# A four-layer decoder on one core: head sums of the narrow attentions sent through DRAM batch by batch, and the last stage's weights built earlier

## The chip, the core and the metric

The kernel runs on one core of a Trainium2 chip. Its engines are TensorE (PE, with its weight load PEld), VectorE (DVE), ScalarE (ACT), GpSimd (POOL) and SyncE (SP), which here issues the transfers. Each engine works through its own instructions in order and waits on semaphores. The metric is the device time of one execution, in microseconds.

## The reference, cut to what matters

Four layers of three sublayers each update `x` (8 batches, 256 tokens, 128 features); every sublayer gets a layer norm of `x` and adds to it. Four of the twelve are attentions with 16 heads of 8 features: two over a context of 512 keys and two causal ones over 256 keys, the last of them gated. All four end like this one, and the last sublayer is a chain of three low-rank-adapted, quantised blocks:

```python
def _L3_xattn_ref(query, key, value, mask, Wq, Wk, Wv, Wo, Wg, bg):
    ...
    scores = jnp.einsum('bhqd,bhkd->bhqk', q, k) / jnp.sqrt(jnp.float32(dk))
    ...
    attn = jax.nn.softmax(scores, axis=-1)
    context = jnp.einsum('bhqk,bhkd->bhqd', attn, v)
    context = context.transpose(0, 2, 1, 3).reshape(B, Sq, D)
    gate = jax.nn.sigmoid(query @ Wg.T + bg)
    return gate * context @ Wo.T

def _L3_ffn_ref(x, qweights, scales, biases, lora_a, lora_b, ln_gamma, ln_beta):
    ...
    h = x
    for blk in range(3):
        i0, i1 = (2 * blk, 2 * blk + 1)
        y = _qlora_linear(h, qweights[i0], scales[i0], biases[i0], lora_a[i0], lora_b[i0])
        y = _layernorm(y, ln_gamma[blk], ln_beta[blk])
        y = jax.nn.gelu(y, approximate=False)
        y = _qlora_linear(y, qweights[i1], scales[i1], biases[i1], lora_a[i1], lora_b[i1])
        h = y + h
    return h
```

## The kernel before, in words

`x` stays in on-chip memory with the features on the partitions and 2048 tokens in columns, worked on as four tiles of 512 columns or eight batches of 256. Each sublayer is one or more blocks of instructions; no engine starts the next block before all have ended the one before.

A narrow attention (`narrow_attention`, L3043) is three stages. `project` (L730) norms `x`, projects queries, keys and values (`unit`), splits them into bf16 parts and stores the first ones in DRAM; at its end SyncE loads the first batch's stacks, while TensorE runs 24 filler matmuls (`keep_clock`). Then `attend_wide` (512 keys, L1151) or `attend_short` (256 keys, L1327) runs nine steps: step s scores batch s ("front") and turns batch s - 1 into logits, exponentials and head sums ("back"). A step goes over the 16 heads, i = 0 to 15. VectorE reduces each score matrix to row maxima. Half a batch's maxima are turned by TensorE, copied by ScalarE and written as further rows of the query stack by two transfers (`place`, L1012 and following); TensorE waits for them at i = 0 and i = 8 (`attend_halves`). SyncE's order in a step is written out in `attend_transfers` (L998): second half of this batch's loads, row maxima, first half of the next batch's loads, row maxima. The sums of four heads make one group; a column group of 32 rows holds a head's eight weighted values and, in the ninth row, the sum of its exponentials. They are copied into `summed`.

After all nine steps `combine` (L1797) handles all eight batches at once: it gathers the denominators by matmuls with constant matrices, inverts them (`reciprocal` of 256 columns, after a guard against zero in the gated stage), gathers the numerators, spreads the inverses, multiplies, and in the gated stage makes the gates (a matmul, a sigmoid and a product on GpSimd), and last it projects and adds to `x`, tile by tile.

The last stage, `lora_ffn` (L2848), loads its weights, dequantises them on GpSimd, builds six 128 x 128 matrices on TensorE (`centre_lora`, `weights`) between and after its norm's steps, and then runs three blocks. In a block each phase goes over all four tiles: `up` into y, ScalarE's squares of all tiles, one square root, one reciprocal, the products z, then per tile a transpose, the Gelu and `down`, and the residual add; the next block's `up` start when all `down` have been issued.

## Time and the profile before

| quantity | value |
|---|---|
| median of 3 runs | 1738.42 us (1737.92 to 1742.84) |
| the profiled execution's own time | 1742.06 us |
| its span | 1740.3 us |
| granted TensorE clock, mean | 0.916 of 2.4 GHz |
| busy | PE 84%, DVE 58%, ACT 46%, POOL 26% |

The span runs from the first to the last instruction of one profiled execution; all times in rows are microseconds from its start unless they say ns. A timeline row has start, length, engine, source line, operation, output and input, count, and in brackets the idle time before it and what ended it. Rows of matmuls count fp32 ones twice. A row of a stretch has its bounds and length, then the busy time and count of PE, PEld, DVE, ACT and POOL, TensorE's granted clock as a share of 2.4 GHz, the share of time that the DMA engines were busy, and the data rate in GB/s.

### The profile page before, as it was taken

To read this page: it belongs to the slowest core of one execution; us is meant where nothing else is said; L and a number is where in the kernel's file an instruction comes from. 1 tells how busy PE (TensorE), PEld (TensorE's weight loads), DVE (VectorE), ACT (ScalarE), POOL (GpSimd) and SP (SyncE) were. 2 spreads that over 40 slices of the span, in tenths; PEclk is the share of its full clock that TensorE was granted. 3 is DMA by queue.
4 is the path that set the end of the run, shared out by engine and by line. 5 is a ranking of instruction groups with operands and counts; after the bars stand their busy time and mean duration, and the time that the engine had idled before them with its cause. 6 is when DMAs were issued, how large, how long until landed. Compare 5 with 4: busy or idle time off the path is not lost. (4 is left out here: it accounts for less than half of the span.)

```text
span 1740.3 us, 30717 instructions
## 1 busy us (share of the span) xinstructions
PE 1470.2 (84%) x10727; PEld 738.2 (42%) x10747; DVE 1009.0 (58%) x1970; ACT 797.1 (46%) x1479; POOL 455.9 (26%) x658
## 2 busy tenths in 40 slices
PE   7998999999749999679876898889836888888887
PEld 5777634444424445246533442222404333433354
DVE  5665598884352222465547578997274574567335
ACT  3554537677213333215330136777434365346535
POOL 6121300000144443320126230000003354245311
PEclk9999999999969999699887898999957899989878
DMA  2000443110200000001000163121001520342000
GB/s 95 1 0 0 146 161 93 42 49 8 117 0 0 1 0 0 0 7 49 5 6 0 57 198 110 50 54 29 15 0 44 169 70 21 98 157 66 11 16 24
DMA packets 82246, 85.67 MB, mean 49 GB/s; under 512 B 7228, under 2 KB 67900, under 8 KB 81756
## 3 DMA queue, kind: packets, MB, share of 16 engines
q1 hardware_dynamic: 82152, 84.45, 15.2%
q8 instruction: 55, 0.90, 0.2%
q14 instruction: 39, 0.32, 0.1%
HBM read 51.33 MB, written 32.51 MB: 48 GB/s over the span
## 5 line engine op out<-in xcount | busy, mean ns | idle before, releaser
L1282 ACT ACTIVATE arena<-ps 128x1024 f32<-128x1024 f32 x256 | 261.9, 1023 | 112.1 <-PE ps L1191 111.2
L1176 PE MATMUL ps<-k_stack,q_stack 49*128 49x512 bf16 x512 | 192.3, 387 | 15.3 <-DVE small L1306 13.2
L1191 PE MATMUL ps<-q_stack,k_stack 51*128 51x256 bf16 x1024 | 191.3, 275 | 0.5 <-ACT arena L1282 0.4
L1303 DVE CUSTOM_DVE_ANT_0 small<-ps,mask_b 128x512 bf16<-128x512 f32 x256 | 168.0, 689 | 33.7 <-PE ps L1176 32.3
L1306 DVE TENSOR_REDUCE small<-ps 128x1 f32<-128x512 f32 x256 | 162.1, 685 | 22.6 <-PE ps L1176 21.6
L1492 DVE TENSOR_REDUCE small<-ps 128x6 f32<-128x768 f32 x128 | 122.6, 958 | 77.8 <-PE ps L1374 75.7
L1203 PE MATMUL ps<-arena,v_pad 128*32 128x256 f32 x2048 | 163.7, 394 | 1.1 <-ACT arena L1282 1.1
L1468 ACT ACTIVATE arena<-ps 128x384 f32<-128x384 f32 x256 | 117.8, 488 | 76.5 <-PE ps L1393 75.8
L1076 POOL TENSOR_SCALAR_AFFINE_SELECT arena<-arena 128x256 f32<-128x256 f32 x256 | 101.9, 406 | 84.2 <-ACT arena L1468 84.0
L2543 DVE TENSOR_TENSOR arena<-ps,arena 128x512 f32<-128x512 f32 x64 | 44.3, 692 | 120.8 <-PE ps L2509 120.8
L2558 POOL TENSOR_TENSOR arena<-arena 128x512 f32<-128x512 f32 x64 | 80.9, 1264 | 108.9 <-DVE arena L2543 107.1
L1183 PE MATMUL ps<-mask_b,ident_b 64*128 64x512 bf16 x512 | 99.8, 382 | 0.5
L1176 PEld LDWEIGHTS ps<-k_stack,q_stack 49*128 49x128 bf16 x512 | 47.7, 94 | 113.2 <-DVE small L1306 82.2
L1049 POOL TENSOR_TENSOR small<-small 128x16 bf16<-128x16 f32 x64 | 13.8, 216 | 312.6 <-DVE small L1309 286.7
L1191 PEld LDWEIGHTS ps<-q_stack,k_stack 51*128 51x128 bf16 x1024 | 75.4, 95 | 29.2 <-issue 6.8
L223 PE MATMUL ps<-xT,mean_w 128*128 128x512 f32 x96 | 56.0, 737 | 24.2 <-DMA xT<-in_xT 4.5
L945 POOL TENSOR_TENSOR arena<-arena 128x512 bf16<-128x512 f32 x40 | 45.5, 1157 | 113.9 <-ACT arena L852 113.9
L238 ACT ACT_TABLE_LOAD x14 | 18.0, 1283 | 113.8 <-PEq L1569 26.2
L2531 ACT ACTIVATE arena<-ps 128x512 f32<-128x512 f32 x64 | 38.2, 597 | 68.9 <-PE ps L2505 65.8
L2505 PE MATMUL ps<-xn,arena 128*128 (+1 forms) x128 | 66.9, 605 | 2.4 <-PEq L2407 2.0
L2490 PE MATMUL ps<-arena 128*128 128x512 f32 x128 | 65.1, 595 | 1.9 <-POOL arena L2558 1.9
L2509 PE MATMUL ps<-xn,arena 128*128 (+1 forms) x128 | 66.3, 599 | 0.0
(353 smaller groups left out, 3036.2 us busy)
## 6 DMA issues: line engine op xcount, KB each, us to landing
q_stack<-q_scratch SPq DMA_DIRECT2D x128, 96.0 KB
k_stack<-k_scratch SPq DMA_DIRECT2D x64, 192.0 KB
k_scratch<-arena SPq DMA_DIRECT2D x8, 768.0 KB, 3.6
k_stack<-k_scratch SPq DMA_DIRECT2D x64, 96.0 KB
q_scratch<-arena SPq DMA_DIRECT2D x4, 1152.0 KB, 5.4
arena<-in_ctxT SPq DMA_DIRECT2D x8, 512.0 KB, 6.6
k_scratch<-arena SPq DMA_DIRECT2D x8, 512.0 KB, 4.7
k_scratch<-arena SPq DMA_DIRECT2D x16, 256.0 KB, 4.5
```

Source lines behind the costliest of these rows:

```text
L1076: pool.affine_select(diag, diag, [[0, 2], [1, P]], ALU.is_ge, 0.0, 0, -1).then_inc(g["masked"].sem, 1)
L1176: pe.matmul(ps[:, t, :], c.q_stack[par][64 * e:64 * e + ROW_MAX, pr, t * P:(t + 1) * P], c.k_stack[par][64 * e:64 * e + ROW_MAX, pr, :], s ...
L1183: return pe.matmul(ps[:, 2 + 2 * (i % 2) + half, :], c.ident_b[r, :], c.mask_b[r, m:m + 2 * S], start=first, stop=False, skip_group_check= ...
L1191: mm = pe.matmul(ps[:, bank, (ch % 2) * S:(ch % 2 + 1) * S], c.k_stack[prv][64 * e:64 * e + ROWS, pr, ch * P:(ch + 1) * P], c.q_stack[prv] ...
L1203: mm = pe.matmul(ps[32 * j:32 * j + 32, 6 + grp % 2, 0:S], c.v_pad[par][:, piece, head_of(i), :], buf.probs[i % 8][:, piece * S:(piece + 1 ...
L1282: act.activation(buf.probs[i % 8], ps[:, bank:bank + 2, :].rearrange("p a n -> p (a n)"), ACT.Exp, scale=scale).then_inc(g["probs"].sem, 1)
L1303: dve.tensor_tensor_reduce(buf.junk[t], ps[:, t, :], c.mask_b[:, M_X + t * SC:M_X + (t + 1) * SC], 1.0, FLOOR, op0=ALU.add, op1=ALU.max, a ...
L1306: dve.tensor_reduce(out, ps[:, t, :], X, ALU.max).then_inc(g["maxed"].sem, 1)
L1468: act.activation(buf.probs[i % 8][:, 0:3 * P], ps[:, 4 + i % 2, 0:3 * P], ACT.Exp, scale=scale)\
L1492: dve.tensor_reduce(buf.m3[par][:, hf, :, pr % HALF, :], ps[:, bank:bank + 2, 0:3 * P].rearrange("p e (a n) -> p e a n", a=3), X, ALU.max)\
L2505: pe.matmul(ps[:, 2 + n % 2, :], w13[:, (ex * 4 + j) * P:(ex * 4 + j + 1) * P], x, start=True, stop=True)\
L2558: pool.tensor_tensor(acts[n % 4][:, :], gated[n % 2][:, :], share_e[n // 2 % 2][:, :], ALU.mult)\
```

## The change

`combine` goes. The head sums of a batch are stored in DRAM as soon as they are complete, with all 32 rows of a head, and come back in another layout: numerators as 128 rows of 256, denominators as 128 rows of 32 columns. VectorE inverts the latter, they are stored again and spread to all rows of a head. These five transfers a batch are issued by SyncE within the attention's steps. From step 4 on ("late") the quotient, the gate, the projection and the add of batch s - 4 lie within step s; in the wide stages the product is on GpSimd and the add goes by way of ScalarE and GpSimd. The last three batches are handled after the steps (`finish_pe`, `finish_act`, `finish_dve`), batch 7 by matmuls instead of transfers. The gate's matmuls and sigmoids move to the end of the projecting stage. The last stage's weights are loaded and built there too (`LoraWeights`), and its three blocks are interleaved tile by tile, with the square root and the reciprocal in two halves. The head order of the output weights and the layout of the constants follow; constants that are needed late are loaded apart. The diff, cut to its core (`LoraWeights.weights` and `dequantise` are as in `lora_ffn` before):

```diff
+            if gated:
+                for t in TS:
+                    if t < 2:
+                        pe.wait_ge(g["ln_scaled"].sem, g["ln_scaled"].at(4))
+                    else:
+                        pe.wait_ge(g["gate_out"].sem, g["gate_out"].at(t - 1))
+                    pe.matmul(ps[:, 2 + t % 2, :], w[:, W_G:W_G + P], norm.tile(c.xn, t), start=True, stop=True)\
+                      .then_inc(g["gate_in"].sem, 1)
+            if ahead:
+                ahead.turn(pe)
...
+            if gated:
+                for t in TS:
+                    act.wait_ge(g["gate_in"].sem, g["gate_in"].at(t + 1))
+                    act.activation(norm.tile(c.xn, t), ps[:, 2 + t % 2, :], ACT.Sigmoid, bias=w[:, W_BG:W_BG + 1])\
+                       .then_inc(g["gate_out"].sem, 1)
+            if ahead:
+                ahead.keep(act)
...
+        with nc.Fori(2, B // 2, 1, engines=[engine]) as it:
+            body(it, 0, True, True, True, True)
+            body(it, 1, True, True, True, True)
+    body(B // 2, 0, False, True, True, True)
...
+    def store_sums(self, buf, sp, b):
+        c, g = self.c, self.c.sig
+        for i in range(2):
+            sp.wait_ge(g[f"summed_out{i}"].sem, g[f"summed_out{i}"].at(2 * b + 2))
+        sp.dma_start(c.sum_scratch[b, :, :, :].rearrange("r j m -> j r m"), buf.summed[:, b, :, :].rearrange("p k n -> p (k n)")).then_inc(g["sums_stored"].sem, 16)
...
+    def spread(self, sp, out, src, sem):
+        sp.dma_start(out, src.unsqueeze(0).to_broadcast([DH, H, S])).then_inc(sem, 16)
...
+    def load_sums(self, sp, b, last=False):
+        c, g = self.c, self.c.sig
+        sem = g[f"sums_back{b % 2}"].sem
+        sp.wait_ge(g["sums_stored"].sem, g["sums_stored"].at(16 * (b + 1)))
+        if b > 1:
+            done, n = self.quotient(b - 2)
+            sp.wait_ge(done.sem, done.at(n + 1))
+        sp.dma_start(self.num[b % 2], c.sum_scratch[b, 0:DH, :, :].rearrange("d j (k n) -> (d j k) n", n=S)).then_inc(sem, 16)
+        if last:
+            self.spread(sp, self.rec[b % 2], c.sum_scratch[b, DH, :, :].rearrange("j (k n) -> (j k) n", n=S), sem)
+        else:
+            sp.dma_start(self.den[b % 2], c.sum_scratch[b, DH, :, :].rearrange("j (a n) -> (j a) n", a=P // 4)).then_inc(sem, 16)
+    def store_inverse(self, sp, b):
+        c, g = self.c, self.c.sig
+        sp.wait_ge(g["inverted"].sem, g["inverted"].at(b + 1))
+        sp.dma_start(c.inv_scratch[b, :, :].rearrange("q (a n) -> (q a) n", a=P // H), self.den[b % 2]).then_inc(g["inv_stored"].sem, 16)
+    def spread_inverse(self, sp, b):
+        c, g = self.c, self.c.sig
+        sp.wait_ge(g["inv_stored"].sem, g["inv_stored"].at(16 * (b + 1)))
+        self.spread(sp, self.rec[b % 2], c.inv_scratch[b, :, :], g[f"inv_spread{b % 2}"].sem)
+    def invert(self, dve, par, half, b):
+        g = self.c.sig
+        dve.wait_ge(g[f"sums_back{par}"].sem, g[f"sums_back{par}"].at(32 * half + 32))
+        if self.guard:
+            dve.tensor_scalar(self.den[par], self.den[par], 1e-30, None, ALU.max).then_inc(g["den_fixed"].sem, 1)
+            dve.wait_ge(g["den_fixed"].sem, g["den_fixed"].at(b + 1))
+        dve.reciprocal(self.den[par], self.den[par]).then_inc(g["inverted"].sem, 1)
+    def divide(self, eng, par, half, done="quotient"):
+        g = self.c.sig
+        eng.wait_ge(g[f"inv_spread{par}"].sem, g[f"inv_spread{par}"].at(16 * half + 16))
+        eng.tensor_tensor(self.quot[par], self.num[par], self.rec[par], ALU.mult).then_inc(g[done].sem, 1)
+    def gate(self, pool, par, b):
+        c, g = self.c, self.c.sig
+        done, n = self.quotient(b)
+        pool.wait_ge(done.sem, done.at(n + 1))
+        pool.tensor_tensor(self.quot[par], self.quot[par], c.xn[:, bass.ds(b * S, S)], ALU.mult).then_inc(g["gated"].sem, 1)
+    def project(self, pe, par, b, bank):
+        c, g = self.c, self.c.sig
+        done, n = (g["gated"], b) if self.gated else self.quotient(b)
+        pe.wait_ge(done.sem, done.at(n + 1))
+        pe.matmul(c.ps[:, bank, 0:S], self.w[:, W_O:W_O + P], self.quot[par], start=True, stop=True, skip_group_check=True)\
+          .then_inc(g["out_proj"].sem, 1)
...
+    def finish_pe(self, buf, pe, scored):
+        c, g = self.c, self.c.sig
+        pe.wait_ge(g["maxed"].sem, g["maxed"].at(scored))
+        pe.wait_ge(g["probs"].sem, g["probs"].at(H * B))
+        self.project(pe, 1, B - 3, 0)
+        self.project(pe, 0, B - 2, 1)
+        for k in range(GROUPS):
+            out = g[f"summed_out{k % 2}"]
+            pe.wait_ge(out.sem, out.at(2 * B - 1 + k // 2))
+            den = pe.matmul(c.ps[0:H, 3, 0:S], c.consts[:, C_DEN + 12 - 4 * k:C_DEN + 12 - 4 * k + H], buf.summed[:, B - 1, k, :],
+                            start=(k == 0), stop=(k == GROUPS - 1), skip_group_check=True)
+            if k == GROUPS - 1:
+                den.then_inc(g["den"].sem, 1)
+            num = pe.matmul(c.ps[:, 4, 0:S], c.consts[:, C_NUM + 3 - k:C_NUM + 3 - k + P], buf.summed[:, B - 1, k, :],
+                            start=(k == 0), stop=(k == GROUPS - 1), skip_group_check=True)
+        num.then_inc(g["num"].sem, 1)
+        keep_clock(c, pe, 6, bank=2)
+        pe.wait_ge(g["inverted"].sem, g["inverted"].at(B))
+        pe.matmul(c.ps[:, 5, 0:S], c.consts[0:H, C_ROWS:C_ROWS + P], self.rec[1][0:H, :], start=True, stop=True, skip_group_check=True)          .then_inc(g["den_spread"].sem, 1)
+        self.project(pe, 1, B - 1, 2)
...
+        def inverse(par, b, rows, den):
+            rec = self.rec[par][0:rows, :]
+            if self.guard:
+                dve.tensor_scalar(rec, den, 1e-30, None, ALU.max).then_inc(g["den_fixed"].sem, 1)
+                dve.wait_ge(g["den_fixed"].sem, g["den_fixed"].at(b + 1))
+                den = rec
+            dve.reciprocal(rec, den).then_inc(g["inverted"].sem, 1)
+        self.divide(dve, 1, B // 2 - 2, "last_quotient")
+        self.add(dve, B - 3, 0)
+        dve.wait_ge(g["sums_back0"].sem, g["sums_back0"].at(16 * B))
+        inverse(0, B - 2, P, self.rec[0])
+        dve.wait_ge(g["inverted"].sem, g["inverted"].at(B - 1))
+        dve.tensor_tensor(self.quot[0], self.num[0], self.rec[0], ALU.mult).then_inc(g["last_quotient"].sem, 1)
+        self.add(dve, B - 2, 1)
+        dve.wait_ge(g["den"].sem, g["den"].at(1))
+        inverse(1, B - 1, H, c.ps[0:H, 3, 0:S])
+        dve.wait_ge(g["num_kept"].sem, g["num_kept"].at(1))
+        dve.wait_ge(g["den_spread"].sem, g["den_spread"].at(1))
+        dve.tensor_tensor(self.quot[1], c.ps[:, 5, 0:S], self.num[1], ALU.mult).then_inc(g["last_quotient"].sem, 1)
+        self.add(dve, B - 1, 2)
...
+        if s > 2:
+            outs.store_inverse(sp, s - 3)
+        if s > 1:
+            outs.store_sums(buf, sp, s - 2)
...
+        if s > 1:
+            outs.load_sums(sp, s - 2, s == B)
+        if s > 2:
+            outs.spread_inverse(sp, s - 3)
...
+        if late and not causal:
+            outs.divide(pool, par, it - 2)
...
+            if late and outs.gated and i == 4:
+                outs.gate(pool, par, s - 4)
...
+        if late and not causal:
+            pool.wait_ge(g["out_kept"].sem, g["out_kept"].at(s - 3))
+            xb = c.xT[:, bass.ds((s - 4) * S, S)]
+            pool.tensor_tensor(xb, xb, outs.kept[par], ALU.add).then_inc(g["residual"].sem, 1)
...
+                    if late and i == 7:
+                        project_late(c, outs, pe, s, par)
...
+                    if late and i == 7:
+                        act.wait_ge(g["out_proj"].sem, g["out_proj"].at(s - 3))
+                        act.activation(outs.kept[par], ps[:, 7, 0:S], ACT.Identity, bias=outs.w[:, W_BO:W_BO + 1])\
+                           .then_inc(g["out_kept"].sem, 1)
...
+                    if n == 2 and s > 2:
+                        outs.invert(dve, 1 - par, (s - 3) // 2, s - 3)
...
+                    if late and pr == 1:
+                        outs.divide(dve, par, it - 2)
+                    if (late or par) and before and pr == 2:
+                        outs.invert(dve, 1 - par, it - 2 + par, s - 3)
+                    if late and pr == 3:
+                        outs.add(dve, s - 4, 7)
...
+class LoraWeights:
...
+    def turn(self, pe):
+        c, g = self.c, self.c.sig
+        pe.wait_ge(g["centring"].sem, g["centring"].at(1))
+        pe.wait_ge(g["lora_in"].sem, g["lora_in"].at(48))
+        pe.wait_ge(g["gate_out"].sem, g["gate_out"].at(T // NT))
+        for i in range(NB):
+            c_matmul(pe, c.ps[:, 2, i * P:(i + 1) * P], self.cols[:, 2 * i:2 * i + 1].to_broadcast([P, P]), self.centring)
+            mm = c_matmul(pe, c.ps[0:LR, 3, i * P:(i + 1) * P], self.turned_up[:, i, :], self.centring)
+        mm.then_inc(g["lora_centred"].sem, 1)
+        pe.wait_ge(g["dequant"].sem, g["dequant"].at(2))
+        pe.wait_ge(g["lora_kept"].sem, g["lora_kept"].at(2))
+        pe.wait_ge(g["ln_std"].sem, g["ln_std"].at(4))
+        self.weights(pe, 0, 4, 4)
+        self.weights(pe, 4, NL, 2)
+    def keep(self, act):
+        c, g = self.c, self.c.sig
+        act.wait_ge(g["lora_centred"].sem, g["lora_centred"].at(1))
+        act.activation(self.up_shift.rearrange("p a n -> p (a n)"), c.ps[:, 2, 0:NB * P], ACT.Identity).then_inc(g["lora_kept"].sem, 1)
+        act.activation(self.up_b[0:LR, :, :].rearrange("p a n -> p (a n)"), c.ps[0:LR, 3, 0:NB * P], ACT.Identity)\
+           .then_inc(g["lora_kept"].sem, 1)
+        for n, i0, i1, bank in ((1, 0, 4, 4), (2, 4, NL, 2)):
+            act.wait_ge(g["turned"].sem, g["turned"].at(n))
+            act.activation(self.wT[:, i0:i1, :].rearrange("p a n -> p (a n)"), c.ps[:, bank, 0:(i1 - i0) * P], ACT.Identity)
...
+            def turn(n, t):
...
+            norm_pe(norm, pe, follow=lambda t: up(0, t))
...
+                for t in range(3):
+                    turn(NTI * blk, t)
+                down(blk, 0)
+                turn(NTI * blk, 3)
+                for t in range(1, 4):
+                    down(blk, t)
+                    if blk < NB - 1:
+                        up(blk + 1, t - 1)
+                if blk < NB - 1:
+                    up(blk + 1, 3)
...
+                    if t % 2:
+                        act.wait_ge(g["ln_square"].sem, g["ln_square"].at(NTI + n + t + 1))
+                        act.activation(half(dev, t // 2), half(ssq, t // 2), ACT.Sqrt, bias=c.consts[:, C_EPS:C_EPS + 1],
+                                       scale=1.0 / D).then_inc(g["ln_std"].sem, 1)
...
+                    residual(blk, t)
+                    if blk < NB - 1 and t:
+                        shift(blk + 1, t - 1)
+                if blk < NB - 1:
+                    shift(blk + 1, 3)
```

## Rows read from the trace of the kernel before

**Rows 1.** Busy time by stretch: third attention's `combine`, and the last stage.

```profile
1470.80:1487.50 16.70, 14.12 (x120) 6.20 (x120) 7.12 (x9) 2.39 (x4) 0.00 (x0) 0.90 0.00 0
1664.70:1740.30 75.60, 60.84 (x283) 42.59 (x284) 33.91 (x88) 38.57 (x135) 7.36 (x6) 0.81 0.07 23
```

**Rows 2.** Busy time by stretch: half steps, masked and unmasked wide; a whole short step.

```profile
312.00:324.90 12.90, 12.85 (x148) 5.38 (x148) 10.73 (x33) 8.99 (x11) 1.05 (x3) 1.00 0.17 46
...
1118.70:1130.00 11.30, 10.24 (x117) 3.29 (x117) 10.22 (x18) 8.78 (x11) 1.05 (x3) 1.00 0.19 53
...
1592.70:1605.60 12.90, 10.94 (x156) 4.41 (x148) 9.16 (x17) 8.25 (x21) 7.51 (x21) 1.00 0.22 64
```

**Rows 3.** Timeline around the first attention's `combine`.

```profile
439.20 1.93 PE L1203 MATMUL ps<-arena,v_pad 128*32 128x256 f32 x32 [0.55 <-ACT arena L1282]
...
445.61 1.76 DVE L1882 RECIPROCAL arena<-ps 128x256 f32<-128x256 f32 x1 [29.85 <-PE ps L1820]
...
455.95 0.75 DVE L1873 SCALAR_TENSOR_TENSOR xT<-ps,att_w,xT 128x512 f32<-128x512 f32 x1 [0.51 <-PE ps L1854]
```

**Rows 4.** Timeline around the gated attention's `combine`.

```profile
1637.56 0.65 PE L1408 MATMUL ps<-arena,v_pad 128*32 128x128 f32 x8
...
1648.21 1.28 ACT L1865 ACT_TABLE_LOAD   x1
...
1652.27 0.69 ACT L1865 ACTIVATE arena<-ps,att_w 128x512 f32<-128x512 f32 x1 [0.17 <-PE ps L1838]
...
1659.03 1.27 POOL L1897 TENSOR_TENSOR arena<-arena 128x512 f32<-128x512 f32 x1 [2.38 <-DVE arena L1886]
...
1663.71 0.75 DVE L1873 SCALAR_TENSOR_TENSOR xT<-ps,att_w,xT 128x512 f32<-128x512 f32 x1 [1.44 <-PE ps L1854]
```

**Rows 5.** Timeline of the gated attention's projecting stage, its end.

```profile
1509.68 5.13 PE L184 MATMUL ps<-mask_b,ident_b 128*128 128x512 bf16 x23
...
1511.29 0.63 ACT L852 ACTIVATE arena<-arena 128x512 bf16<-128x512 f32 x1 [0.37 <-DVE arena L898]
...
1518.49 0.59 PE L184 MATMUL ps<-mask_b,ident_b 128*128 128x512 bf16 x2 [3.69 <-PEq L770]
```

**Rows 6.** Timeline of two norms: a bare one, and the start of another.

```profile
460.33 5.37 PE L223 MATMUL ps<-xT,mean_w 128*128 128x512 f32 x8 [4.42 <-PEq L2398]
...
472.88 0.69 DVE L269 TENSOR_TENSOR xn<-arena,ps 128x512 f32<-128x512 f32 x1 [0.20 <-PE ps L205]
...
1487.59 3.67 PE L223 MATMUL ps<-xT,mean_w 128*128 128x512 f32 x8 [1.11 <-PEq L1811]
```

**Rows 7.** Timeline of the last stage: the building of its weights.

```profile
1674.93 2.23 PE L205 MATMUL ps<-arena 128*128 128x128 f32 x12
...
1677.59 0.46 ACT L2957 ACTIVATE arena<-ps 32x384 f32<-32x384 f32 x1
...
1691.37 0.39 PE L2907 MATMUL ps<-arena 128*128 128x128 f32 x2
...
1694.70 0.60 ACT L2962 ACTIVATE arena<-ps 128x512 f32<-128x512 f32 x1 [0.26 <-PE ps L2908]
```

**Rows 8.** Timeline of the last stage: its three blocks.

```profile
1688.05 0.69 DVE L3003 TENSOR_TENSOR arena<-ps,arena 128x512 f32<-128x512 f32 x1 [1.02 <-PE ps L205]
...
1694.76 3.23 DVE L3010 TENSOR_SCALAR arena<-arena,small 128x128 f32<-128x128 f32 x16
...
1709.46 0.25 DVE L3006 RECIPROCAL small<-small 128x16 f32<-128x16 f32 x1 [2.51 <-ACT small L2982]
...
1726.43 0.25 DVE L3006 RECIPROCAL small<-small 128x16 f32<-128x16 f32 x1 [2.50 <-ACT small L2982]
...
1736.69 0.75 DVE L3017 SCALAR_TENSOR_TENSOR xT<-ps,arena,xT 128x512 f32<-128x512 f32 x1 [0.39 <-PE ps L2950]
```

**Rows 9.** The page's DMA issues, and SyncE's own in the gated steps.

```profile
k_scratch<-arena SPq DMA_DIRECT2D x16, 256.0 KB, 4.5
...
L960 SPq DMA_DIRECT2D k_stack<-k_scratch x24: 443/446/1080, 1541.3 to 1613.8; - x24
```

More of the change, by code:

```diff
@@ L951, in project @@
         g.advance(**{f"ctx_in{t}": 16 for t in TS})
+    if gated:
+        g.advance(gate_in=T // NT, gate_out=T // NT)
+    if ahead:
+        ahead.advance()
 def load_stacks(c, sp, par, hf, q_at, k_at, nk, key_mask_at=None):
@@ L1058, in attend_pool, with step @@
     pool.wait_ge(g["cleared"].sem, g["cleared"].at(1))
-    def step(it, par, front, back, before):
+    def step(it, par, front, back, before, late):
         s = it * 2 + par
@@ L1207, in sum_piece, with step @@
                     mm.then_inc(g["summed"].sem, 1)
-            def step(it, par, front, back, before):
+            def step(it, par, front, back, before, late):
                 first = isinstance(it, int) and it == 0
@@ L1313, in _ @@
                 step(s)
+            outs.invert(dve, 1, B // 2 - 2, B - 3)
+            outs.finish_dve(dve)
+    outs.advance()
+    g["out_kept"].advance(B - LAST)
     if masked:
@@ L1394, in logits, with sum_piece @@
                       .then_inc(g["logits"].sem, 1)
-            def sum_piece(grp, piece, b, par, first, front=True):
+            def sum_piece(grp, piece, b, par, first, front=True, late=False):
                 if piece == 0:
-                    sum_waits(c, pe, grp, b, first, front, "masked")
+                    sum_waits(c, pe, grp, b, first, front, late, "masked", "residual")
                 for j in range(4):
@@ L1410, in sum_piece, with step @@
                     mm.then_inc(g["summed"].sem, 1)
-            def step(it, par, front, back, before):
+            def step(it, par, front, back, before, late):
                 first = isinstance(it, int) and it == 0
@@ L2852, in lora_ffn @@
+def lora_ffn(c, weights):
     nc, g, ps = c.nc, c.sig, c.ps
@@ L2994, in _, with shift, residual @@
         def _(dve):
-            dve.tensor_tensor(centring, c.ident[:, :], c.mean_w[:, :], ALU.subtract).then_inc(g["centring"].sem, 1)
+            def shift(blk, t):
+                dve.wait_ge(g["up"].sem, g["up"].at(NTI * blk + t + 1))
+                dve.tensor_tensor(fold(y[:, t, :], (4, P)), fold(ps[:, t, :], (4, P)),
+                                  up_shift[:, blk, :].unsqueeze(1).to_broadcast([P, 4, P]), ALU.add).then_inc(g["y_kept"].sem, 1)
+            def residual(blk, t):
+                dve.wait_ge(g["down"].sem, g["down"].at(NTI * blk + t + 1))
+                if blk == NB - 1:
+                    dve.wait_ge(g["summed"].sem, g["summed"].at(t + 1))
+                h = norm.tile(c.xT if blk == NB - 1 else c.xn, t)
+                dve.scalar_tensor_tensor(h, ps[:, t, :], cols[:, 2 * blk + 1:2 * blk + 2], h, ALU.add, ALU.add)\
+                   .then_inc(g["residual"].sem, 1)
```

429 lines of the change are left out of this document (173 added, 256 removed).

## The prediction

> **What bounds the kernel now.** The profiled execution took 1742.06 us (span 1740.30); the median of the runs is 1738.42. The sum below is made in the frame of the profile and its difference is carried over to the median. The page's chain of waits reaches back only through the last stage, so I read stages instead: the boundaries from the timeline, then busy time by stretch, then single rows. The reader should see four attention stages with a serial tail (`combine`) and a last stage that nothing overlaps. Within the attention loops TensorE is the bound: in half a step of the masked wide loop it is busy 12.85 of 12.90 us, in half a step of the unmasked one 10.24 of 11.30 with VectorE at 10.22, in a whole step of the short one 10.94 of 12.90 [rows 2]. In the tails the bound is a chain that hops between engines: the `combine` of the third attention holds 16.7 us in which TensorE's records cover 14.1 but VectorE 7.1 and ScalarE 2.4 [rows 1]; the last stage, 75.6 us, has no engine over 61 us, at a granted clock of 0.81 [rows 1].
>
> **The change, part by part.**
>
> *1. The tails.* Now: from the end of the last head-sum matmuls (439.20 + 1.93 = 441.1) to the last residual add (455.95 + 0.75 = 456.7), 15.6 us in a wide stage [rows 3]; about 17.3 in the third attention (the window of 16.7 and a good half us of copy ahead of it) [rows 1]; 1638.2 to 1664.5, 26.3 us, in the gated one [rows 4]. After: batches 0 to 4 leave within the loop, and `finish_pe` and `finish_dve` handle three. Its order matters. TensorE projects batch 5, VectorE adds it, and only then does VectorE invert batch 6's 256 columns; a reciprocal of 256 columns costs 1.76 us whatever the rows [rows 3]. `finish_pe` issues the projection of batch 6 ahead of batch 7's eight sum matmuls, so those wait for it although their data is there. One full-width fp32 matmul of 512 columns takes 3.67 / 4 = 0.92 us at full clock, close to 0.86 start to start, so one of 256 takes 0.43 [rows 6]. Chain: projection 0.65 with its latency, add 0.4 (half of 0.75), reciprocal 1.76, product 0.45: 3.3 us. Nine matmuls: 3.9. Then reciprocal 1.76, spread 0.65, product 0.45, projection 0.65, add 0.4: 3.9. Sum 11.1 us at full clock.
> But TensorE is idle for nearly 3 us in the first piece. After 4.42 us idle the norm's eight matmul records took 5.37 us, after 1.11 us idle 3.67 [rows 6]: the stretch began at 1.2 GHz. I add the same 1.7 us to the nine matmuls and 0.3 for the second gap, under the last reciprocal: 13.1 us per tail. (The Trainium skill, TensorE: Matmul & The Clock Gate, What's actually happening, says that the throttled state is the default and activity releases it; by it the six filler matmuls, which come only after the sums, can't help those sums. By that rule the tail is 13.1, without it 11.1.) Saved: 2.5 in each wide stage, 5 in all, between 4 and 9. Third attention: 17.3 - 13.7 (batch 5's spread reciprocals may land half a microsecond late) = 3.5, between 1 and 5.5. Gated: 13.7, two guards at about 0.45 and two Pool gates of 256 columns at half of 1.27 plus a handover [rows 4], 16.1; saved 10, between 8 and 13. Gate matmuls and sigmoids are gone from it. Sum of part 1: 18.5.
> The norm after the third attention now starts 1.11 us after dense matmuls and runs at full clock. After the change it follows a sparse tail: +1.7 (5.37 - 3.67) [rows 6]. The other norms start at half clock already.
>
> *2. In the loops.* In four steps per stage that also score, TensorE gets a projection of 256 columns: 0.43, where it is the bound. ScalarE's extra 256-column copy and Pool's product and add in the wide loops hide in their slack (ScalarE 8.8 of 11.3, Pool 1.1 [rows 2]). VectorE gets one reciprocal of 32 columns per step: between 0.25 (16 columns) [rows 8] and 1.76 (256), by the slope 0.35; in the short loops a product and an add of 0.4 each too, under a busy time of 9.1 of 12.9 [rows 2]. In the unmasked loop both engines stand near 10.2 of 11.3, and part of it shows. In the short loops Pool also gates (0.65) ahead of the masking that the sums wait for. I take 0.5 us a step: 2 us a stage, 8 us in all; from 4 (half of TensorE's share hides) to 14 (every addition of TensorE and VectorE shows).
> The five transfers a batch cost SyncE five issues of about 0.45 us [rows 9]. In the gated short loop it has twelve loads and four row-maximum transfers a step, 9.1 us by the same row and its waits, so 11.4 with the new ones, of a step of at most 12.9 [rows 2]: just under. The data (512 KB out, some 290 KB back, twice as much as half a step's loads) meets DMA engines busy 0.22 of the time [rows 2]; a landing is 4.5 us [rows 9], and each has a third of a step or more. I cost them at nothing; the cover is the order of SyncE's queue. Without it, batch sums come late to VectorE's in-order reciprocal, and what is late next is the reduce behind it and so the scores.
>
> *3. The gated projecting stage.* It now ends when SyncE has issued its loads: TensorE ends its filler at 1514.8 and waits 3.69 us for the block's end, until 1518.5 [rows 5]. That slack is all the cover. The new work stands in TensorE's queue ahead of the 24 filler matmuls, and they stay. ScalarE is done at 1511.9 [rows 5]. Table load and four sigmoids with their matmuls: 1648.21 to 1652.96, 4.75 us [rows 4], to 1516.7. Twelve small matmul records 2.2 and two copies, 3.1 us (1674.9 to 1678.05) [rows 7], to 1519.8. Weights: four of them 3.4 us at full clock (1691.3 to 1694.7), 0.85 each [rows 7]; I take six at 1.07, partly at half clock, 6.4, to 1526.2. Filler 5.3 (5.13 for 23) [rows 5], to 1531.5. Block end and next start, 0.4: 1531.9 against 1518.5. Cost +13.4; all at full clock 12, with half clock throughout the weights and gates 17. The five weight transfers are issued in SyncE's idle time after the context's, and Pool's dequantising ends before its first part is due: nothing. All of the next stage shifts, since its own transfers are issued from its start.
>
> *4. The last stage.* Norm: centring and weights are gone from it. A bare norm runs from 460.33 to 473.6, 13.2 us [rows 6]; with the four `up` (0.93 each) woven in between its products, VectorE's first shift ends at +16.5 after the stage's start. Now it ends at 1688.74 - 1664.74 = +24.0 [rows 8]. Saved 7.5. Blocks: now 17.0 from reciprocal to reciprocal (1709.46 to 1726.43) and 15.0 for the first pair; the last add ends at 1737.44 [rows 8]. After: from a block's first shifted tile, two tiles of squares 2.6, square root 0.3, reciprocal 0.25; the other two squares go on, so the second root ends at +5.5 to 6.0 instead of all before the one root; table load and first Gelu input 1.5, at +7.5; Gelu 0.78; `down` 0.93 and residual 0.75, then `up` 0.93 and shift 0.7 for tile 0: the next block's first shifted tile at +12.7. The z products (3.23 for 16 [rows 8]) of the first half are now under the squares. Three blocks: 12.7 + 12.7 + 12.8 = 38.2; after 16.5, the end at +54.7 against +72.7: 18 saved if TensorE has its full clock. It idles some 4 us in every block, and its turns can go at half clock; I take off 2: 16 saved, between 12 and 18.
>
> *5. The rest.* Later constants, split loads and one more unrolled pair of steps: nothing, the load is not waited for where it stands.
>
> **Sum.** 18.5 + 16 - 8 - 1.7 - 13.4 = 11.4 us less: 1742.06 - 11.4 = 1730.7 in the profile's frame, 1727 against the median of 1738.42. 0.3% (5.2 us) is about what a measurement of this kernel can tell from no change.
>
> **Rivals.**
> A (slower): *the transfers share one in-order queue with the row maxima.* TensorE waits for each batch's maxima at every half step. If the stores or SyncE's waits push those back, every step from the third on pays. From 0.6 us a step in all 28 steps, or 1.2 in the 14 short ones, the 11.4 are gone and the time is over 1743.6. At 1 us each: 1727 + 28 = 1755. For it: short steps leave SyncE only about 1.5 us. Against: no DMA wait in a steady step of the masked loop (12.85 busy of 12.90) and a DMA share near 0.2 [rows 2]. (The Trainium skill, DMA: Bandwidth & Descriptors, on the fixed part of a transfer, gives about 2.0 us; four dependent ones would be an estimated 8 us and more, which two steps hold.) Chance 0.13.
> B: *the projecting stage costs what the last stage gives.* Weights and gates at half clock (17), blocks at 14.5 us each (12 saved): 7.6 less gained, 1734.5, no measurable change. Chance 0.18.
> C: *cheap everywhere.* Loops 4, tails at full clock, projecting 12: 1714. For it: the short loops' slack. Chance 0.14.
> D: *the tails don't shrink*, because the first three-batch chain waits on transfers of the last step (each some 4 us): 3 us more in each, 1739. Chance 0.05.
> Forecast as summed, 1720 to 1733: 0.50.
> Range: from near C to between D and A, 1714 to 1741. Faster 0.68 (forecast, C, part of B), same 0.18, slower 0.14.
>
> **What the profile after would show.** The l3x attention begins 12 to 17 us later after its projecting stage starts, with matmuls of the last stage's weights and then the filler ahead of it. Tails of about 13 us in wide stages, 16 in the gated one, with a TensorE gap of some 3 us under a 1.76 us reciprocal. Late steps 0.3 to 0.8 us longer. The last stage 57 to 60 us to its end. I am wrong if row-maximum transfers appear as releasers in steady steps, if VectorE's 32-column reciprocal waits on a DMA, or if the projecting stage ends with SyncE as before.

## Result: 7.1% slower, and the profile after

The changed kernel takes 1861.63 us (median of 4 runs, 1859.1 to 1866.2), the kernel before 1738.17 us beside it (4 runs). The ratio is 1.071, with a 95% interval of 1.0678 to 1.0743. Forecast were 1727 us, within 1714 to 1741.

Where the 124.2 us between the two profiled spans (1864.5 and 1740.3) arise, by the first transfer or matmul of each stage in the timelines; two later kernels stand beside them:

| stage | before | after | difference | after, store in four (e1) | before with the last stage's part, no filler (e6) |
|---|---|---|---|---|---|
| start to the first wide attention | 180.1 | 182.2 | +2.1 | 182.1 | 182.1 |
| first wide attention, masked | 276.9 | 283.2 | +6.3 | 280.3 | 279.4 |
| stages up to the second | 532.8 | 535.7 | +2.8 | 535.0 | 529.5 |
| second wide attention | 257.7 | 269.5 | +11.8 | 256.8 | 255.9 |
| quantised block | 76.3 | 77.3 | +1.0 | 74.5 | 74.6 |
| third attention (short steps) | 163.7 | 216.7 | +52.9 | 172.9 | 166.5 |
| gated attention (short steps) | 177.2 | 239.1 | +61.9 | 196.2 | 176.8 |
| last stage | 75.6 | 60.9 | -14.6 | 60.4 | 59.9 |

The last stage did what was forecast. 115 us are lost in the two stages with short steps. By stretches, columns as in [rows 1] (four short steps of the third attention; the gated projecting stage; the last stage to its last add):

```profile
1433.20:1514.50 81.30, 60.15 (x602) 21.82 (x605) 39.96 (x75) 33.55 (x80) 31.00 (x85) 0.75 0.32 81
1564.40:1613.00 48.60, 43.93 (x188) 26.32 (x188) 14.87 (x29) 20.25 (x35) 11.41 (x10) 0.86 0.31 93
1803.50:1861.97 58.47, 48.11 (x240) 33.47 (x240) 33.62 (x90) 37.26 (x134) 5.09 (x4) 0.86 0.03 12
```

A short step holds 20.3 us where [rows 2] had 12.90 at most, and no engine is busy for more than 15.04 (60.15 / 4) of them, at a granted clock of 0.75. The work has not grown by 7 us; something is waited for. In these four steps TensorE waits 16.8 us in all for row maxima, four waits of at most 5.2; and behind them it runs for a while at the lower of its two clock levels, so that a wait costs more than it lasts: with the same work its busy time is 11.64 us a step in e1 below, at a granted clock of 1.00, against 15.04 here. TensorE's largest entry in the list of waits of the whole span (total, times, longest), and SyncE's largest from 1455 to 1580, the end of the third attention:

```profile
PE ps L1594 <- DMA q_stack<-max_rows: 50.0, 10, 7.4
```

```profile
SPq L1072 <- DMA sum_scratch<-arena: 21.3, 5, 9.4
SPq L1578 <- PEq L1578: 17.9, 1, 17.9
SPq L1212 <- ACT max_rows L1326: 16.0, 5, 6.2
SPq L1082 <- DVE small L1097: 7.1, 4, 1.8
```

TensorE's entry is the row maxima, which the prediction named as a sign that it was wrong, and which rival A was about. SyncE's timeline of one short step:

```profile
1474.13 1.29 SPq L1212 DMA_DIRECT2D q_stack<-max_rows  x2
1477.23 0.34 SPq L1082 DMA_DIRECT2D inv_scratch<-small  x1
1477.68 0.57 SPq L1058 DMA_DIRECT2D sum_scratch<-arena  x1
1479.42 0.31 SPq L992 DMA_DIRECT2D q_stack<-q_scratch  x1
1479.78 2.07 SPq L992 DMA_DIRECT2D k_stack<-k_scratch  x1
1481.90 1.10 SPq L992 DMA_DIRECT2D q_stack<-q_scratch  x1
1483.04 0.73 SPq L992 DMA_DIRECT2D k_stack<-k_scratch  x1
1483.82 1.29 SPq L1212 DMA_DIRECT2D q_stack<-max_rows  x2
1488.40 0.34 SPq L1072 DMA_DIRECT2D arena<-sum_scratch  x1
1488.79 0.43 SPq L1076 DMA_DIRECT2D small<-sum_scratch  x1
1489.26 0.67 SPq L1062 DMA_DIRECT2D arena<-inv_scratch  x1
...
1494.32 1.29 SPq L1212 DMA_DIRECT2D q_stack<-max_rows  x2
```

The reader is to see three things. The store of the sums (L1058) is issued at 1477.68, and SyncE, which waits for its landing at L1072, gets on at 1488.40, 10.7 us later. The load issues right behind the store take up to 2.07 us instead of 0.45: something holds up the queue. And the row-maximum pairs are 9.7 and 10.5 us apart instead of some 6.3. So there were two candidates: the store itself, and SyncE's dependent waits.

### The profile page after: what moved, and what is told of

The parts are those of the page before. It is cut to its first block and busy times, and to the rows that moved or that the text cites. A ratio compares the mean times of both kernels' runs of the same rounds, so it can differ in the third digit from the quotient of the medians.

```text
span 1864.5 us, 29754 instructions
## 1 busy us (share of the span) xinstructions
PE 1534.1 (82%) x10419; PEld 752.1 (40%) x10419; DVE 1024.5 (55%) x2020; ACT 795.4 (43%) x1480; POOL 473.5 (25%) x682
## 5 line engine op out<-in xcount | busy, mean ns | idle before, releaser
L1509 ACT ACTIVATE arena<-ps 128x1024 f32<-128x1024 f32 x256 | 262.2, 1024 | 126.4 <-PE ps L1415 126.1
L1400 PE MATMUL ps<-k_stack,q_stack 49*128 49x512 bf16 x512 | 193.9, 389 | 21.2 <-DVE small L1538 11.9
L1415 PE MATMUL ps<-q_stack,k_stack 51*128 51x256 bf16 x1024 | 193.0, 276 | 0.5 <-ACT arena L1509 0.4
L1538 DVE TENSOR_REDUCE small<-ps 128x1 f32<-128x512 f32 x256 | 163.7, 686 | 31.1 <-PE ps L1400 29.6
L1594 PE MATMUL ps<-mask_b,ident_b 128*128 128x256 bf16 x256 | 62.5, 336 | 66.7 <-DMA q_stack<-max_rows 50.0
L1250 POOL TENSOR_TENSOR small<-small 128x16 bf16<-128x16 f32 x64 | 13.8, 216 | 310.9 <-DVE small L1543 286.3
L1630 PE MATMUL ps<-q_stack,k_stack 51*128 51x256 bf16 x256 | 77.6, 346 | 0.0
L1613 PE MATMUL ps<-k_stack,q_stack 49*128 49x256 bf16 x256 | 75.0, 333 | 0.0
```

The source lines that it names most:

```text
L1400: pe.matmul(ps[:, t, :], c.q_stack[par][64 * e:64 * e + ROW_MAX, pr, t * P:(t + 1) * P], c.k_stack[par][64 * e:64 * e + ROW_MAX, pr, :], s ...
L1415: mm = pe.matmul(ps[:, bank, (ch % 2) * S:(ch % 2 + 1) * S], c.k_stack[prv][64 * e:64 * e + ROWS, pr, ch * P:(ch + 1) * P], c.q_stack[prv] ...
L1509: act.activation(buf.probs[i % 8], ps[:, bank:bank + 2, :].rearrange("p a n -> p (a n)"), ACT.Exp, scale=scale).then_inc(g["probs"].sem, 1)
L1538: dve.tensor_reduce(out, ps[:, t, :], X, ALU.max).then_inc(g["maxed"].sem, 1)
L1630: pe.matmul(ps[:, bank, 0:S], k[:, 0:P], q, start=True, stop=True, skip_group_check=True)
```

## The experiments

Ratios are to the kernel before on the same chip, with their 95% intervals in brackets.

**e1 and e2: the same data in four stores.** The single store has a destination pattern of 4 x 32 x 1024, with the 4 slowest.

```diff
-        sp.dma_start(c.sum_scratch[b, :, :, :].rearrange("r j m -> j r m"), buf.summed[:, b, :, :]...)
+        for j in range(4):
+            sp.dma_start(c.sum_scratch[b, 0:32, j, :], buf.summed[32 * j:32 * j + 32, b, :, :]...)
```

(e2 has 16 in place of 32 rows: half the bytes, all that is read back.)

> The changed kernel, with the 512 KB store of a batch's head sums issued as four transfers of 32 rows of 4 KB instead of one whose slowest dimension is 4; same bytes, same place in SyncE's order, same waits. Theory 1 (the single store is worked on by few DMA engines, so it lands only some 10.7 us after its issue, and SyncE, which waits for that landing ahead of the next loads and row maxima, passes the delay on): the store lands in about 4 us, the steps of the two short loops fall from 20.6 us to 14 to 15, the whole to 1765 to 1790. Theory 2 (the length of the dependent chain of waits in SyncE's queue, whatever the store): steps stay at 19 to 21, the whole above 1840. Theory 3 (the number of bytes): no change but three more issues of 0.45 us, about 1865.

> As the run with four stores of 32 rows, but only the first 16 rows of each head's 32 are stored (nine are read back): half the bytes. Theory 1: within 10 us of the run with 32 rows, 1755 to 1785. Theory 2: above 1840 like that one. Theory 3 (bytes): half of the loss of the two short loops comes back against the run with 32 rows, about 1810.

Measured: e1 1764.35 us, 1.0142 [1.0027, 1.0257]; e2 1764.98 us, 1.0145 [1.0043, 1.0248]. By the medians some 97 of the 124 us are gone (e1's interval alone leaves 20 us either way; e8 and e14, built on it, come out at 1.0161 and 1.0137) with the same bytes, the same place in the queue and the same waits, and half the bytes change nothing more. Theories 2 and 3 fall. SyncE's timeline of a short step in e1, and four of its steps by stretch:

```profile
1441.01 1.28 SPq L1213 DMA_DIRECT2D q_stack<-max_rows  x2
1442.39 0.34 SPq L1073 DMA_DIRECT2D arena<-sum_scratch  x1
...
1447.47 1.29 SPq L1213 DMA_DIRECT2D q_stack<-max_rows  x2
1449.72 0.34 SPq L1083 DMA_DIRECT2D inv_scratch<-small  x1
1450.17 1.77 SPq L1059 DMA_DIRECT2D sum_scratch<-arena  x4
1452.05 0.37 SPq L992 DMA_DIRECT2D q_stack<-q_scratch  x1
1452.46 0.46 SPq L992 DMA_DIRECT2D k_stack<-k_scratch  x1
...
1454.98 1.28 SPq L1213 DMA_DIRECT2D q_stack<-max_rows  x2
```

```profile
1413.50:1468.60 55.10, 46.55 (x608) 18.75 (x600) 40.31 (x77) 33.69 (x81) 30.88 (x84) 1.00 0.48 113
```

SyncE no longer waits for the landing (L1073 follows the row maxima at once, and a store's landing is 2.2 us by the page), load issues are back at 0.45, the clock is 1.00 and the step 13.8 us.

**e3, e4, e9, e10: the store alone, in the kernel before.** Each adds one transfer of 512 KB a step behind `place(s - 1, 1)`, of columns of x that don't change; nothing waits for it before the stage's end. Only the shape of the destination differs.

```diff
             place(s - 1, 1)
+        if s > 1:
+            sp.dma_start(c.sum_scratch[s - 2, :, :, :].rearrange("r j m -> j r m"), c.xT[:, 0:GROUPS * S])...
```

> The kernel before, with one more transfer a step from step 2 on: 512 KB to DRAM, with the changed kernel's access pattern (slowest dimension 4), right behind the row maxima of the second half; it stores columns of x that nothing changes here, and nothing waits for it. Theory 1 in its narrow form (only SyncE's wait for the landing counts): no more than 2 us a short step for a fuller queue, 1742 to 1760. Theory 1 in its wide form (row maxima and loads use the same few DMA engines and queue up behind the store even without a wait): 5 us or more in each of 14 short steps, above 1800. Theory 2: 1740 to 1745.

> The same added transfer to the kernel before, but with 128 rows as its slowest dimension. By either form of theory 1: 1738 to 1750, well under the run whose slowest dimension is 4 if the wide form holds. If bytes count (theory 3): as long as that run.

> The kernel before with the same added 512 KB transfer a step that nothing waits for, its destination pattern now of 8 x 16 x 1024 with the 8 slowest. If the slowest dimension sets how many DMA engines work on a transfer, it lands in about half the time of the one with 4, some 5 us, and costs the short steps little: 1738 to 1760, against 1806 with 4. If it is the permuted order of the rows in DRAM that makes it slow, as much as with 4: about 1806.

> As that run, with 16 x 8 x 1024 and the 16 slowest: permuted like the pattern with 4, but divisible by 16. If the slowest dimension decides: the landing is near the 2.7 us of the unpermuted store and the time that of the kernel before, 1733 to 1745. If the permuted order decides: about 1806.

| slowest dimension of the destination | time, us | ratio | landing by the page |
|---|---|---|---|
| 4 (e3) | 1806.11 | 1.0382 [1.0277, 1.0487] | none given |
| 8 (e9) | 1757.03 | 1.0094 [1.0064, 1.0124] | none given |
| 16, rows permuted (e10) | 1746.03 | 1.0028 [1.0007, 1.0048] | 3.7 us |
| 128, rows in order (e4) | 1736.70 | 0.9986 [0.9946, 1.0026] | 2.7 us |

The same 512 KB cost 66 us, 16, 5 or nothing (the ratio less one, times 1739), by the pattern alone. The interval of the 66 reaches from 48 to 85 us, and those of the last two rows overlap, so that a price of the permuted order by itself is not shown. (e10 missed its range of 1733 to 1745 by 1 us and its landing of 2.7 by 1.) The rest goes with the slowest dimension. How the DMA engines work on it, in 30 us of short steps (the row DMA is their mean busy share in 40 slices, in tenths), e3 first, then e4:

```profile
DMA  2555324268000000001226135562245811000000
...
sum_scratch<-xT SPq DMA_DIRECT2D x1, 512.0 KB
```

```profile
DMA  4957800000076200029506730000007630007900
...
sum_scratch<-xT SPq DMA_DIRECT2D x2, 512.0 KB, 2.7
```

With 4 slowest the engines are about a quarter to a half busy on average over 7 to 11 us at a time; with 128, in bursts of two to five slices that reach 0.9, with idle time between. TensorE in e3 waits for the same transfers as in the changed kernel (list of waits, four and a half short steps):

```profile
PE ps L1360 <- DMA q_stack<-max_rows: 9.7, 3, 4.0
...
PE ps L1360 <- DMA k_stack<-k_scratch: 7.4, 1, 7.4
```

Read together: a few engines carry the whole store, and the row maxima, 4 KB a transfer, and the loads come to lie behind it. The delay without any wait is measured; that it comes from shared engines is the reading that fits the table and the DMA rows. (The Trainium skill, DMA: Bandwidth & Descriptors, Why a DMA increments its semaphore by 16 and not by 1, says that a transfer issued by SyncE runs on the largest number of engines up to 16 that divides the slowest dimension of both its patterns, and on the lowest-numbered ones. By it the store has four engines, and the row maxima, whose destination has two rows slowest, two of the same four. The order 4, 8, 16 of the table agrees; which engine carried what no run here shows.) It would have been the rule to weigh in the prediction.

**e12: the wait for the landing, by itself.** e3, and SyncE waits for the store's landing behind `place(s, 0)`, where the changed kernel does.

```diff
+        if s > 1:
+            sp.wait_ge(g["sums_stored"].sem, g["sums_stored"].at(16 * (s - 1)))
```

> The kernel before with the added 512 KB store whose slowest dimension is 4 (1806 without a wait), and SyncE waits for its landing behind the row maxima of the first half, where the changed kernel does. If the wait is the other part of the loss of the short loops (their steps: 20.6 us in the changed kernel, 17.0 with the store alone), steps near 20 and 1830 to 1850. If the wait is nearly free because the queue is held up anyway: 1806 to 1815, and the rest of the changed kernel's loss is its own work and its other transfers.

Measured: 1804.17 us, 1.0359 [1.0307, 1.0411], like e3. So the wait is nearly free here, and by the reading above it should be: the row maxima placed just before it lie behind the same store, so TensorE would wait in any case. With e3's 66 us without any wait, the narrow form of my theory is refuted. But the wait is shorter here than in the changed kernel: 6.7 us in four and a half short steps (1400 to 1480) against 13.5 in four (1433.2 to 1514.5), where the store is issued later. That the longer one is free too is not shown.

**e13, e14, e15: the rest of the short loops.** By the medians e3 explains 66 us and e1 leaves 25; 33 of 124 are still open. e13 (the changed kernel) and e14 (e1) move the store of the reciprocals behind the row maxima; e15 adds to e3 two reads a step that nothing waits for, shaped like those of the numerators and of the spread reciprocals.

```diff
-        if s > 2:
-            outs.store_inverse(sp, s - 3)
         if s > 1:
             outs.store_sums(buf, sp, s - 2)
 ...
             place(s, 0)
+        if s > 2:
+            outs.store_inverse(sp, s - 3)
```

> The changed kernel with its single store, but the store of the reciprocals (for which SyncE waits on VectorE) stands behind the row maxima of the first half instead of ahead of the store of the sums. If that wait (the store of the sums is issued 3.5 us after the row maxima in the changed kernel, 1.3 us in the kernel before with the store added) holds up the whole queue: 1 to 2 us less in each of 14 short steps, 1835 to 1850. If the reads and the broadcast behind the store are the rest: within 5 us of 1862.

> The same move in the version with four stores of 32 rows (1764). There no engine waited for a transfer in steady short steps, so the order in the queue shouldn't count: 1760 to 1768. If SyncE's wait still held up row maxima: 1745 to 1755.

> The kernel before with the added store whose slowest dimension is 4 (1806), and behind the first half's row maxima two reads that nothing waits for: 128 KB with 128 rows slowest, and a broadcast of 16 KB to 128 rows, whose slowest dimension is 8. If the sums' own reads behind the store are the other part: 1820 to 1840. If not: 1804 to 1812.

Measured: e13 1854.83 us, 1.0616 [1.0584, 1.0647]; e14 1771.12 us, 1.0137 [1.0107, 1.0166]; e15 1812.66 us, 1.0374 [1.032, 1.0428]. The chip of these three was slower (before: 1747.89), so ratios count: e13 takes 0.94% or some 16 us off the changed kernel, e14 nothing off e1, e15 adds nothing to e3. In the changed kernel SyncE waited for VectorE's reciprocal ahead of the store and issued it 3.55 us after the row maxima; now it is 2.3 to 2.5 us, and steps are 18.9 us long:

```profile
1451.28 1.30 SPq L1212 DMA_DIRECT2D q_stack<-max_rows  x2
1453.55 0.57 SPq L1058 DMA_DIRECT2D sum_scratch<-arena  x1
...
1459.75 1.29 SPq L1212 DMA_DIRECT2D q_stack<-max_rows  x2
```

A late issue matters only where what stands behind it lands late. Of the third attention's 52.9 us, 9.2 are left in e1, e3 shows 30.9 for the store (stage 194.6), e13 takes away 8.0 (208.6); 4.8 stay open, if the parts add up. By the step they nearly do: e3's short steps are 17.6 us long, the changed kernel's own work is 1.1 (e1), e13's steps are 18.9, and the late issue is the rest of 20.3. The 11.8 of the second wide attention, which neither e1 nor e3 (258.3) has, lie in its first late steps; the list of waits from 1089 to 1131 of the changed kernel has

```profile
PE ps L1400 <- DMA k_stack<-k_scratch: 6.5, 1, 6.5
```

There the store is issued 4.5 us after the row maxima (1093.95 against 1089.45, since it waits for the last sums), and three stores of key parts and the loads follow it. That reading was not tried by itself.

**e5, e6, e11, e7: the last stage's part alone, in the kernel before.** e5 takes over `LoraWeights` and the interleaved blocks; attentions, `combine` and gates stay. e6 also drops the 24 filler matmuls of that projecting stage; e11 is the same kernel timed again; e7 also has the gates moved as in the change.

```diff
-            keep_clock(c, pe, PARTS_WAIT, bank=bank_of(kind, n))
+            keep_clock(c, pe, 0 if ahead else PARTS_WAIT, bank=bank_of(kind, n))
```

> The kernel before, with only the last stage's part of the change: weights loaded and built in the gated projecting stage, blocks interleaved tile by tile; attentions, combine and gates as before. From the stages of the changed kernel: last stage 61 us instead of 75.6 (14.6 saved), projecting stage 17 us longer of which about 5.5 were the gates, so 11.5 lost: about 3 us less than before, 1733 to 1738. If the last stage's gain had depended on the changed attention ahead of it, 1745 or more.

> As the run before it, without the 24 filler matmuls at the end of the gated projecting stage, since the weights' matmuls now stand there. If the filler only comes on top (it took 6.4 us in the changed kernel, from 1606.54 to 1612.95, and nothing else was under way): 6 us less than that run, 1727 to 1732. Rival: the attention then begins at half clock and gives 2 to 4 us of it back, or SyncE's loads end later than the weights: 1731 to 1735.

> As the run without filler, and the gates' matmuls and sigmoids moved from combine to the projecting stage as the change has it; combine multiplies by them as before. Costs about 5.5 us in the projecting stage, saves at most 4.75 in combine if they stand in its chain: from 1 less to 5 more than the run without filler. If the gates lay beside other work in combine, 5 more.

> The same kernel as the run with the last stage's part alone and no filler, timed longer, since it is the version that beats both: 0.994 of the kernel before, between 0.991 and 0.997, 1725 to 1732.

Measured: e5 1734.02 us, 0.9984 [0.9961, 1.0007]; e6 1727.17 us, 0.9940 [0.9919, 0.9960]; e11 1723.37 us, 0.9903 [0.9878, 0.9928]; e7 1731.34 us, 0.9963 [0.9939, 0.9986]. e6 and e11 are the version that beats both kernels; e11 came out just below its range. Leaving the filler out gave 0.44% or 7.6 us between e5 and e6, about the 6.4 that it took. In e6 the weights' matmuls end, and the attention begins, like this:

```profile
1517.13 0.80 PE L2919 MATMUL ps<-ident,arena 128*128 128x128 f32 x2
1517.86 0.79 PE L2920 MATMUL ps<-arena 32*128 32x128 f32 x2
1519.36 1.01 PE L184 MATMUL ps<-mask_b,ident_b 128*128 128x512 bf16 x2 [0.71 <-PEq L770]
```

From its first transfer at 1487.91 that is 31.4 us, as before (1487.55 to 1518.49, 30.9 [rows 5]): without gates and filler the weights fit into SyncE's slack. The attention does begin at the lower clock level, as the rival in the expectation had it (granted clock 0.50 from 1519.3 to 1522), but the filler had not bought much in the kernel before either, where TensorE idles 3.69 us behind it (0.61 from 1518.4 to 1521). e7's gates in front of the weights cost some 4 us more than they save in `combine`, though the intervals of e6 and e7 touch.

**e8: the same filler out of e1.**

> The changed kernel with four stores of 32 rows a batch and without the filler in the gated projecting stage. About 6 us less than the run with the filler (1764): 1755 to 1760, still slower than before by what the short steps (1.1 us each in 14) and the gates cost.

Measured: 1763.33 us, 1.0161 [1.0112, 1.0209], against 1.0142 [1.0027, 1.0257] for e1. No gain can be told from that, which was not expected; its attention begins at 1548.07, 42.6 us after its projecting stage (1505.46), where e1 takes 46.1 (1501.57 to 1547.64). So 3.5 us are there in the stage, and the scatter of the rest hides them.

## Why the prediction was wrong, by its own steps

**Step 2 failed, at its last term:** "I cost them at nothing; the cover is the order of SyncE's queue." It summed issue time (five times 0.45 us) and took a landing of 4.5 us from [rows 9], whose transfer has 128 rows as its slowest dimension. The new store has four. It landed after 10.7 us in a short step, and what the cover left out is that the row maxima and loads issued behind it land late even if nothing waits for the store. By e3 the store alone is 66 us, by e1, which changes nothing else, 97 in the whole kernel. Rival A had the place and the sign (one queue shared with the row maxima), with chance 0.13 and a price of 1 us a step; short steps grew by 7.6 (20.3 against 12.7), 1.1 of it their own work by e1, and steady masked wide ones are 26.4 us with either store. Its argument against, no DMA wait and a low DMA share, was drawn from the wide loop, where the landing took 10.7 us too (329.32 to 340.00) but half a step of 12.9 holds it; half a short step of 6.3 does not. And a DMA share is a mean over sixteen engines: in e3 it was 0.29 (1400 to 1480) against 0.22 in [rows 2], and TensorE waited all the same.

The rest of step 2 was 0.5 us in each late step. e1 shows it without the store's effect: masked wide 0.7 (26.4 against 25.7), unmasked 0.7 too (23.3 us from row maxima to row maxima against 22.6), short 1.1 (13.8 against 12.7 in the third attention). In the short steps TensorE is 0.7 us a step busier than in [rows 2] (46.55 / 4 = 11.64 against 10.94): the 256-column projection takes 0.61 to 0.71, not the 0.43 costed.

**Step 1, the tails,** held in the wide stage and missed in the short ones. Wide, from the last sums' end (451.13) to the last add's (465.05): 13.9 us, against 13.1 forecast and 15.6 before [rows 3]. The gap under the first reciprocal and the half clock behind it are there (timeline of the first wide tail):

```profile
452.20 1.74 DVE L1168 RECIPROCAL xn<-xn 128x256 f32<-128x256 f32 x1
...
454.46 0.71 PE L1117 MATMUL ps<-xn,att_w 128*128 128x256 f32 x2 [2.70 <-DVE xn L1175]
...
455.11 1.04 PE L1139 MATMUL ps<-arena,consts 128*16 128x256 f32 x2
...
458.92 0.61 PE L1139 MATMUL ps<-arena,consts 128*16 128x256 f32 x2
```

The matmul of 0.61 us takes 1.04 behind the gap, until 458.3. (The Trainium skill, TensorE: Matmul & The Clock Gate, What's actually happening, has the throttled state as the default, which activity releases; the trace agrees: the granted clock was 0.62 from 454.4 to 458.9 and 1.00 from there to 462.6.) Third attention: 19.3 us (1544.9 to 1564.2) against 13.7 forecast and 17.3 before; gated: 22.9 (1780.3 to 1803.2) against 16.1 and 26.3. In both VectorE waits for batch 5's inverses (5.67 us in the third attention, 5.24 in the gated one), whose last transfer SyncE issues only behind its wait for the landing of the last step's store:

```profile
1783.66 0.43 DVE L1103 TENSOR_TENSOR arena<-arena 128x256 f32<-128x256 f32 x1 [5.24 <-DMA arena<-inv_scratch]
```

That is rival D's mechanism, on top of A. In e1 they are 17.4 and 18.0 us: rival D still holds in the third attention (VectorE waits 2.83 us for the inverses), where nothing is saved, while the gated tail gives back 8.3 of the 10 forecast.

Its last term, the norm behind the third attention, was right: the mean's eight matmul records took 5.27 us (from 1564.53) where 5.37 was forecast.

**Step 3, the gated projecting stage,** was the right mechanism with sizes a little small: 48.7 us (1564.50 to 1613.2) against 30.9, +17.8 where 13.4 and that norm's 1.7 make 15.1. TensorE's timeline from the last gate matmuls on:

```profile
1591.93 3.53 PE L854 MATMUL ps<-xn,att_w 128*128 128x512 f32 x4 [2.63 <-ACT xn L906]
...
1605.82 0.79 PE L3036 MATMUL ps<-arena 32*128 32x128 f32 x2
1606.54 6.41 PE L188 MATMUL ps<-mask_b,ident_b 128*128 128x512 bf16 x24
1613.25 0.59 PE L188 MATMUL ps<-mask_b,ident_b 128*128 128x512 bf16 x2 [0.30 <-PEq L775]
```

From ScalarE's last part (1589.87) to its last sigmoid (1596.18) are 6.3 us for 4.75, in which TensorE waits 2.63 for ScalarE; weights 7.1 for 6.4, filler 6.4 for 5.3. In e1 the stage costs +15.1 (46.1), as forecast.

**Step 4, the last stage,** was right: the first shifts end 16.4 us after its start (forecast 16.5), the last add at +58.1 (forecast 54.7, and 56.7 with the 2 us that were taken off the saving), 14.6 saved for 16. VectorE's rows, from the shifts on:

```profile
1819.25 2.48 DVE L3157 TENSOR_TENSOR arena<-ps,arena 128x512 f32<-128x512 f32 x4
1822.78 0.20 DVE L3175 RECIPROCAL small<-small 128x8 f32<-128x8 f32 x1 [1.05 <-ACT small L3143]
...
1832.44 0.69 DVE L3157 TENSOR_TENSOR arena<-ps,arena 128x512 f32<-128x512 f32 x1
...
1846.28 0.69 DVE L3157 TENSOR_TENSOR arena<-ps,arena 128x512 f32<-128x512 f32 x1
...
1859.15 2.47 DVE L3166 SCALAR_TENSOR_TENSOR xT<-ps,arena,xT 128x512 f32<-128x512 f32 x3 [0.75 <-PE ps L3116]
```

Blocks are 13.2, 13.8 and 14.7 us long where 12.7 was forecast. e5 shows step 4, and step 3 but for its gates, without the attentions: 0.9984, no measurable change, so the projecting stage eats most of the last stage's gain, as rival B had it; only without the filler do they pay.

**Step 5** held: the first attention's start is 2.1 us later, inside the scatter of that stretch (below).

With e1, the steps can be judged without the failed term. Its span is 17.9 us over that of before (1758.2 against 1740.3) where 11.4 less was forecast, so 29.3 are missing. By the table, 10.7 of them lie in the third attention (+9.2 where -3.5 + 2 was forecast) and 11.9 in the gated one (+19.0 for 15.1 - 10 + 2), in loops that cost 1.1 us a step instead of 0.5 in four of them, their first steps, and the tails above. The other 6.7 are spread over stages where single profiles scatter as much. How the short loops' part divides between TensorE's and VectorE's added work was not tried.

## What to carry to other kernels

Read the shape of a transfer, not only its bytes: name the slowest dimension of both sides, and take a landing only from a row of the same shape. Before adding a transfer to a queue that others wait behind, ask what those others need of the DMA engines, above all where a step is shorter than the landing; a store split so that many rows stand slowest cost four issues and gave 97 us back. Filler that was put in to keep the clock in a gap should go when real work fills the gap (e6 against e5; between e8 and e1 no gain could be told).

## What the runs showed of the hardware that was not expected

- The same 512 KB store, waited for by nothing, costs 66, 16, 5 or 0 us over 28 steps with 4, 8, 16 or 128 as its destination's slowest dimension.
- Waiting for that store's landing on top cost nothing in the kernel before (1.0359 against 1.0382), 6.7 us of SyncE's time in four and a half steps though it was. In the changed kernel the same wait tops SyncE's list with 21.3 us.
- The page gives no landing time for the stores with 4 or 8 slowest, nor for the row maxima and the spread reciprocals, and one for the stores with 16 or 128. But it gives none either for the loads of the stacks (48 rows) and for the late constants (128 rows, 143.5 KB), so a missing time alone doesn't tell a narrow transfer.
- The start of the first wide attention, with the same code ahead of it in all kernels made from the kernel before, came at 178.9 us (e4) to 188.1 us (e15) in single profiles: of a single profile's differences in that stretch, 9 us mean nothing.
